# The order of the first stage of an attention-and-FFN kernel: demodulation rows, norms, folded matrix and first value projection against the first scores

## The reference, cut to what matters

```python
x = x * s1[:, None, :]
x = (x - mu) * jax.lax.rsqrt(var + EPS_IN)
q = heads(jnp.einsum('bsh,oh->bso', x, q_weight) * q_dc[:, None, :])
k = heads(jnp.einsum('bsh,oh->bso', x, k_weight) * k_dc[:, None, :])
v_flat = jnp.einsum('bsh,oh->bso', x, v_weight) * v_dc[:, None, :] * s2[:, None, :]
attn = jax.nn.softmax(jnp.einsum('bhqd,bhkd->bhqk', q, k) * scale, axis=-1)
out = jnp.einsum('bhqk,bhkd->bhqd', attn, v).transpose(0, 2, 1, 3).reshape(B, S, H)
out = jnp.einsum('bsh,oh->bso', out, w_weight) * w_dc[:, None, :]
skip = jnp.einsum('bsh,oh->bso', v_flat, u_weight) * u_dc[:, None, :]
return x_in + ffn(out + skip)   # ffn: int8 product with absmax scales
```

## Time and profile before

| what | us |
|---|---|
| median of three runs (lowest, highest) | 430.51 (429.87, 430.66) |
| profiled execution | 430.85 |
| its span | 429.0 |
| PE busy in the span | 406.4 |
| ACT, DVE, POOL busy | 294.9, 279.0, 107.4 |

### The profile page before, as it was taken

How to read it: one execution, slowest core, us unless ns; L and a number is a source line. 1 busy time by engine, 2 the same in 40 slices (tenths; PEclk the granted TensorE clock), 3 DMA queues, 4 the chain that set the end, 5 groups by cost and what they waited for, 6 DMA issues and landing times.

```text
span 429.0 us, 7595 instructions
## 1 busy us (share of the span) xinstructions
PE 406.4 (95%) x2544; PEld 216.7 (51%) x2544; DVE 279.0 (65%) x634; ACT 294.9 (69%) x341; POOL 107.4 (25%) x115
## 2 busy tenths in 40 slices
PE   8886989999999999999999999999999999999894
PEld 7773625354544455454445554445545545453273
DVE  7645468455984778566875588477856656547355
ACT  2533378868777687867786787868786878787811
POOL 7175204100231023500523023502350052102201
PEclk9996889999999999999999999999999999999999
DMA  5399225723475426622586326621773157602021
GB/s 164 111 137 135 26 101 103 132 70 98 72 127 108 107 70 130 170 74 98 113 133 158 99 68 131 174 81 63 141 172 74 37 109 125 163 0 99 2 98 49
DMA packets 29327, 44.19 MB, mean 103 GB/s; under 512 B 3880, under 2 KB 15144, under 8 KB 29256
## 3 DMA queue, kind: packets, MB, share of 16 engines
q1 hardware_dynamic: 27040, 38.31, 40.8%
q0 software_dynamic: 1040, 3.70, 2.7%
q10 hardware_dynamic: 1200, 1.59, 2.4%
HBM read 14.17 MB, written 4.25 MB: 43 GB/s over the span
## 4 chain that ended last, share of the span: by engine, by line
PE 79%; DVE 8%; ACT 4%; DMA 3%; issue 3%; SPq 1%; POOL 0%; DVEq 0%; POOLq 0%
PE o_acc L1088 26%; PE scores L1074 18%; PE work L1139 12%; PE work L1116 8%; PE work L1200 5%; ACT probs L557 4%; DMA k_stack<-parts 2%; PE work L1127 2%; PE work L1355 2%; PE work L1243 1%; DMA rows<-in_cond_dram 1%; SPq L293 1%; PE work L1229 1%; PE work L1215 1%; PE work L1051 1%
## 5 line engine op out<-in xcount | busy, mean ns | idle before, releaser
L557 ACT ACTIVATE probs<-scores 128x1024 f32<-128x1024 f32 x256 | 247.5, 1024 | 82.4 <-PE scores L1074 82.4
L1088 PE MATMUL o_acc<-probs,v_aug 128*32 128x512 f32 x1024 | 124.4, 604 | 0.0
L1074 PE MATMUL scores<-q_stack,k_stack 50*128 50x512 f32 x512 | 98.2, 455 | 8.5 <-ACT probs L557 5.7
L1074 PEld LDWEIGHTS scores<-q_stack,k_stack 50*128 50x128 f32 x512 | 39.9, 186 | 81.0 <-ACT probs L557 63.3
L1088 PEld LDWEIGHTS o_acc<-probs,v_aug 128*32 128x32 f32 x1024 | 26.9, 110 | 60.4 <-issue 57.0
L1139 PE MATMUL work<-vs_w,x_t 128*128 128x512 f32 x192 | 52.9, 420 | 0.0
L438 POOL TENSOR_TENSOR squares<-parts 128x512 bf16<-128x512 f32 x30 | 31.3, 1042 | 68.2 <-ACT parts L541 68.2
L694 DVE TENSOR_TENSOR v_aug<-work,rows 128x128 f32<-128x128 f32 x64 | 15.6, 286 | 45.8 <-PE work L1139 45.2
L1139 PEld LDWEIGHTS work<-vs_w,x_t 128*128 128x128 f32 x192 | 35.7, 196 | 15.9 <-issue 7.2
L1116 PE MATMUL work<-x_t,qk_w 128*128 128x512 f32 x168 | 43.0, 404 | 0.0
L446 POOL TENSOR_TENSOR res<-res,x_res 128x512 f32<-128x512 f32 x15 | 19.1, 1280 | 90.8 <-DVEq L837 90.8
(11 more groups left out here) (161 smaller groups left out, 442.9 us busy)
## 6 DMA issues: line engine op xcount, KB each, us to landing
q_stack<-parts SPq DMA_DIRECT2D x96, 128.0 KB, 3.8
k_stack<-parts SPq DMA_DIRECT2D x88, 128.0 KB, 4.0
x_res<-in_x_dram SPq DMA_DIRECT2D x8, 512.0 KB, 4.4
x_sb<-in_x_dram SPq DMA_DIRECT2D x7, 512.0 KB, 5.1
out_dram<-res POOLq DMA_DIRECT2D x7, 512.0 KB, 4.7
rows<-rows_dram SPq DMA_DIRECT2D x7, 384.0 KB, 4.1
rows<-in_cond_dram SPq DMA_DIRECT2D x8, 128.0 KB, 4.9
k_stack<-parts ACTq DMA_DIRECT2D x8, 128.0 KB, 9.7
```

Source lines behind the costliest of these rows:

```text
L557: nc.scalar.activation(probs[:, r % RING, pair:pair + 2, :], scores[:, pair:pair + 2, :], ACT.Exp).then_inc(exp_done, 1)
L1074: last = nc.tensor.matmul(scores[:, 2 * (u % 2) + e, :], k_stack[top:top + ROWS, t % 2, head, kt * P:(kt + 1) * P], q_stack[top:top + ROWS ...
L1088: last = nc.tensor.matmul(o_acc[DV * j:DV * (j + 1), :], v_aug[:, kt, 4 * g + j, :], probs[:, r % RING, 2 * (j % 2) + j // 2, :], start=(k ...
```

## The change

- PE: the six transposes of `demod` come first, then the dummy matmuls (five, into `o_acc`), then the norms, also in `o_acc`, so that they take no `work` bank. Skip matrix, transposed maximum, `rows_of_first` and `values(0, 0)` follow, all before the flag is read and before the first scores. `values(0, 1)` stands between the scores of rounds 0 and 1, and `values(0, 2)` is all that is left of the fill of step 0.
- ACT: copies the two rows banks (L586 of the new file) in place of DVE. It no longer issues the four DMAs with the high part of k for group 1, and loads the table of the exponential behind the rounding of the skip matrix.
- SP: issues those four DMAs, between the last q loads and the last two k loads of group 1.
- DVE: `modulate(1)` stands between the low parts of group 0 and the sums, `measure()` behind the reciprocal. The maximum of the norms comes before the last low part. The rest of the skip matrix, the copies of batch 0's rows and `v_and_skip(0, 0)` come before the branch. `normalise_x(1)` comes before `v_and_skip(0, 2)`.
- POOL: `inverse_root(1)` comes before the two memsets.

```diff
-        return [[("row", 0, 0), ("row", 0, 1), ("v", t, 0), ("v", t, 1), ("v", t, 2)],
+        return [[("v", t, 0), ("v", t, 1), ("v", t, 2)],
...
-    ORDER = [("cond", 0, 0), ("sums", 0, 0), ("xt", 0, 0), ("xt", 0, 1), ("sums", 0, 1), ("norms", 0, 0), ("fold", 0, 0),
-             ("rows", 0, 0), ("rows", 0, 1)]
+    ORDER = [("cond", 0, 0), ("sums", 0, 0), ("xt", 0, 0), ("xt", 0, 1), ("sums", 0, 1), ("rows", 0, 0),
+             ("rows", 0, 1), ("fold", 0, 0), ("row", 0, 0), ("row", 0, 1)]
...
+        def norms_bank(a):
+
+            return o_acc[:, :] if a == 0 else work[:, USE[("norms", a, 0)] % NW, :]
...
             load_stack(0, 2, 1)
+            load_stack(0, 3, 0)
             load_stack(0, 3, 1)
...
             scale_values(0)
+            inverse_root(1)
             nc.gpsimd.memset(k_stack[:, 1, :, :].bitcast(F32), 1.0).then_inc(k_cleared, 1)
             nc.gpsimd.memset(q_stack[:, 1, :, :].bitcast(F32), 0.0).then_inc(q_cleared[1], 1)
-            inverse_root(1)
...
-            act.wait_ge(hi_ready, 4)
-            act.sem_inc(spare, 1)
-            load_first_keys(3, 0)
-            load_first_keys(3, 2)
-
-            nc.scalar.activation(table[:, :], ones[:, 0:1], ACT.Exp)
+            for n in range(2):
+                use = USE[("rows", 0, n)]
+                act.wait_ge(work_ready, use + 1)
+                ms = slice(0, 2) if n == 0 else slice(2, 3)
+                nc.scalar.activation(demod_rows[:, ms, :], work[0:B, use % NW, 0:(2 - n) * H].rearrange(
+                    "b (m o) -> b m o", m=2 - n), ACT.Copy).then_inc(demod_rows_ready, 1)
+                act.wait_ge(demod_rows_ready, n + 1)
+                act.sem_inc(work_freed, 1)
             use = USE[("fold", 0, 0)]
             act.wait_ge(work_ready, use + 1)
             nc.scalar.activation(vs_w[:, 0, :, H:2 * H], work[:, use % NW, :].rearrange("p (c o) -> p c o", c=HC), ACT.Copy
                                  ).then_inc(first_hi, 1)
+
+            nc.scalar.activation(table[:, :], ones[:, 0:1], ACT.Exp)
...
             low_part(0, 1)
+            modulate(1)
             sums(1, other_chunks)
             dve.wait_ge(root_ready, 2)
             nc.vector.reciprocal(demod[:, other_chunks, :], demod[:, other_chunks, :]).then_inc(inverse_ready, 1)
+            measure()
...
             low_part(0, 2)
+            largest_norms(0)
             low_part(0, 3)
-            largest_norms(0)
             bound_flag(0)
...
-            row_shift(0)
-            modulate(1)
-            measure()
...
             dve.sem_inc(first_rows, 1)
+            v_and_skip(0, 0)
+            row_shift(0)
...
-                    v_and_skip(t, 0)
                     v_and_skip(t, 1)
+                    normalise_x(1)
                     v_and_skip(t, 2)
-                    normalise_x(1)
...
-            pe.wait_ge(work_freed, USE[("norms", 0, 0)] - NW + 1)
-            keep_clock(work[:, USE[("norms", 0, 0)] % NW, :], 6)
-            norms(0)
-            norms_transposed(0)
-            skip_matrix(0)
             pe.wait_ge(demod_ready, 1)
...
-            row_maxima(0, PROLOGUE_USES)
+            pe.wait_ge(wu_ready, 1)
+            keep_clock(norms_bank(0), 5)
+            norms(0)
+            skip_matrix(0)
+            norms_transposed(0)
+            rows_of_first()
+            values(0, 0)
+            row_maxima(0, USE[("v", 0, 0)] + 1)
...
                     scores_of(r)
+                    if r == 0:
+                        values(0, 1)
```

More of the change, by code:

```diff
@@ L1144, in norms @@
                 pe.wait_ge(squares_ready, a * 4 + 4)
-                bank = claim("norms", a, 0)
+                bank = norms_bank(0) if a == 0 else claim("norms", a, 0)
                 for n in range(4):
@@ L1153, in norms_transposed @@
                 pe.wait_ge(norms_ready, a + 1)
-                bank = work[:, USE[("norms", a, 0)] % NW, :]
-                transpose(bank[0:1, 0:P], norm_max[:, :]).then_inc(work_ready, 1)
+                transpose(norms_bank(a)[0:1, 0:P], norm_max[:, :]).then_inc(first_norms if a == 0 else work_ready, 1)
             def row_maxima(a, uses_done):
@@ L1279, in fill @@
                 if i == 0:
-                    if first:
-                        rows_of_first()
-                        values(t, 0)
-                    values(t, 1)
+                    if not first:
+                        values(t, 1)
                     values(t, 2)
```

25 lines of the change are left out of this document (11 added, 14 removed).

## The result

The changed kernel takes 424.18 us in the median of four runs (422.6 to 426.85), the kernel before beside it 430.19 (429.62 to 430.66): a ratio of 0.9856, 95% interval 0.9827 to 0.9885. The median of all nine is 423.26; the forecast was 423.3. That it is met so closely is luck, since single runs lie up to 3.6 us from it and the first four have their median 0.9 above it.

What follows compares the result with a forecast made beforehand. PE bounds the kernel, busy 95% of the span; in the first slices its waits, order and half clock do. Profiled 430.85 less 7.2 gives 423.65; lowered for the profile lying 0.34 above the median: 423.3 us, range 421.3 to 426.8.

Steps and rivals of the forecast that it cites:

- Skip matrix at 29.81: PE's skip matrix keeps its start of 29.81 us, following POOL's scaled wv at 29.50; bounds 0 and +1.
- Rival 1: The clock falls between skip matrix and `values(0, 0)`: most likely 1.65 us lost, 424.9, up to 428.3; chance 0.30.
- Flag and the rest of the skip matrix: Flag written 1.52 us after the transposed maximum starts, at 33.3; rest of skip matrix done at 34.0, `values(0, 0)` at 34.2.
- The branch: PE's flag read and branch ahead of the first scores: 0.1 us, mostly hidden by `values(0, 0)`; bounds 0 and 1.8.
- First scores: First scores on PE start at 35.9 us against 35.08 before, 0.8 later.
- Value matmuls: Value matmuls of round 0 start at 41.2 us instead of 48.36.
- rival 3: First scores late through style row, open branch or group 0's landing: 424.3 to 425.5; sign, scores after 36.5; chance 0.08.
- The sum: Value matmuls of round 0 start 7.2 us earlier, and the whole kernel gains that 7.2 us.
- rival 2: The second half-clock stretch, 59.4 to 62.7 us, vanishes too: 1.6 us more gained, 421.7; chance 0.18.
- The edits that cost nothing: Copies on ACT, table load, one dummy less, `inverse_root(1)`, `normalise_x(1)` and SP's extra DMAs add nothing to the time.
- The four DMAs: Moving ACT's four k loads brings group 0 forward under 0.3 us, landing 34.7 to 35.0, 0.9 ahead of first scores.
- Rival 4: SP's fuller queue delays the store of the rows and x of batch 2, passing the gain on: 432.0; chance 0.05.

Runs made afterwards that it cites:

- warm_before: The kernel before with ten dummy matmuls added behind the transposes of `demod`, in PE's wait for the stacked operands: 431.15 us, ratio 1.0018.
- second execution: Profiled execution of the changed kernel, unedited, from its later measurement on another chip: 422.16 us; that measurement's median 423.07 us, ratio 0.9831.
- queue_undone: The changed kernel with the four high-part k loads of group 1 issued by ACT again: 422.59 us, ratio 0.9837.
- store_flag: The changed kernel with SP storing the rows ahead of the last two k loads, and DVE's flag behind the rest of the skip matrix: 423.62 us, ratio 0.9842.
- order_alone: The kernel before with only the projections reordered, and DVE's copies of batch 0's rows and `v_and_skip(0, 0)` ahead of its branch: 427.9 us, ratio 0.9948.
- between_undone: The changed kernel with `values(0, 1)` again behind the scores of round 1: 424.4 us, ratio 0.9866.
- order_undone: The changed kernel with spread rows and value projections behind the first scores again, and DVE's branch ahead of batch 0's row copies: 431.55 us, ratio 1.0005.
- warm_before_2: The kernel before with ten dummy matmuls behind the transposes of `demod`, the same kernel measured a second time: 429.78 us, ratio 0.9965.
- pauses_undone: The changed kernel with batch 1's `modulate` and `measure` behind DVE's branch again, and `inverse_root(1)` behind the memsets: 422.56 us, ratio 0.9828.

## Why the prediction was right, point by point

- **What bounded the stretch.** Right in kind. Of the time between first scores and value matmuls of round 0, 13.2 us, the new order leaves 5.24. The clock's part, read from rows 4, was tested only in part, since it fell in that test too: 2.6 us by `warm_before`'s trace.
- **Skip matrix at 29.81.** 29.90 in the second execution, 31.09 in the first. That DVE would not make POOL late holds (`modulate(1)` took 1.56 in its new place rather than 1.22, the sums started at 23.47 in the first), but the scaled wv was not what the skip matrix waited for: it was there at 28.55 and 28.79, and PE came late, so that 29.90 is near the forecast by luck. What was missed is a fall of the clock in the projections *before* it. In `queue_undone`, without that fall, the same 12 matmuls took 3.06, and the skip matrix followed POOL's product (to 28.93) at 28.98, 0.8 ahead of the forecast. Rival 1 put the fall between skip matrix and value projection and was given 0.30; there the clock was 1.00 in all nine executions with the change's order and its parts around it. It fell at 22 to 29 instead in three of the nine, at a price of 2.3 us in those 12 matmuls of the first (5.32 less 3.06); its skip matrix came 1.3 later than forecast.
- **Flag and the rest of the skip matrix.** Mis-sized: the flag was written 1.15 us after the transposed maximum's start, not 1.52. `values(0, 0)` began 3.82 after the skip matrix, forecast 4.4. These 0.6 us were won.
- **The branch.** Taken at 0.1 between 0 and 1.8: 0.18. `store_flag` fits the other bound, 1.82 from flag to scores, when the cover is gone.
- **First scores.** Forecast 35.9: 35.58 and, with the slow projections, 36.77. **Behind them** 5.3: 5.24 and 5.22. **Value matmuls** forecast 41.2: 40.82 and 41.99. The first execution shows a sign of rival 3, scores behind 36.5, but for none of its reasons: neither style row nor branch nor DMA was late, the clock was.
- **The sum.** 7.2 forecast; by the chain 6.3 in the first execution (0.9 less: 1.3 lost ahead of the skip matrix, and 0.4 won behind it, the 0.6 of the flag less 0.2 in the branch and in rounding) and 7.5 in the second. Then 0.5 was given back in the first (the value matmuls at 53 took 3.52, those before 3.18, and a few tenths are unaccounted for), while in the second the fall at 53 did not come at all: that is rival 2, and the milestone moved to -8.7. So the 7.2 stand for what runs with different falls of the clock give on average, and not for a sum of which each term came true. Forecast and rival 2 are two draws of one kernel, not two possible kernels.
- **The edits that cost nothing.** They cost nothing, but the text did not say what they are worth. It treated copies on ACT as neutral, when more than half of the sum hung on the parts around the order: with the transposes behind the skip matrix and DVE's copies, the spread rows do not lie in the wait for it, and `order_alone` gets 3.0 us.
- **The four DMAs.** Group 0 of `k_stack` landed about 34.9 in `between_undone`, without ACT's four, and about 34.5 in `queue_undone`, with them; forecast 34.7 to 35.0 (35.37 in `store_flag`). So the queue of the four does not matter, as the sum had it. The margin of 0.9 to the first scores does not always hold: with a skip matrix at 28.98 or 29.31 these two executions have PE ready for the scores as the DMA lands, and `between_undone` waits 0.15 us for it. The 3 to 4 us that the prediction took from the round-robin between queues were misread: ACT's four for group 1 stand on their queue behind its four for group 0, so they could take from SP's queue only what was left once those had moved. In `queue_undone` ACT's queue had moved 0.52 MB, its group 0, by 32 us, at the end 0.13 MB in each 2 us beside 0.13 and 0.12 on SP's; then nothing from 32 to 34, though its last four DMAs were issued by 29.2, beside 0.26 on SP's; then 0.13 again beside 0.14. The equal shares agree with the Trainium skill's rule (DMA: Bandwidth & Descriptors, Queues, rings and completion order) that a DMA engine goes round-robin between the queues that have work. By that rule group 0 would have gained half of the 3 us from 32 to 35, some 1.5 us (an estimate), and not 3 to 4. It gained nothing that shows, since ACT's queue moved next to nothing then (0.02 MB from 32 to 34); no run here shows why.
- **Rival 4.** Out as a threat, as the Trainium skill's rule that spreading DMAs over issuing engines brings no bandwidth would have it (DMA: Bandwidth & Descriptors, Rules for kernel authors). The trace agrees: from 36 to 38 us SP's queue alone moved 0.27 MB in the changed kernel's first trace, SP's and ACT's together 0.26 in the kernel before. The store landed at 46.3 in the second. Present as 0.62 us of PE's time.

## What to carry to other kernels

Work that needs nothing of a late operand belongs ahead of the first instruction that waits for it, and the next such piece between two steps that share buffers with a slower engine; both waits are found by asking what ended PE's idle time. Before such a move is priced, list who makes its inputs and what stands before them on that engine: here the move alone gave 3.0 us, and 6 to 7.8 with the parts around it, of which moving two copies from DVE to an idle ACT is the one that the wait points at. Where a flag is read to a register in front of the next step, as here, some 1.8 us of other work have to cover it; shortening the chain in front of it by pushing the flag back gained nothing.

## What the runs showed of the hardware that was not expected

- The granted clock falls at different places in executions of one program: 12 to 17 in thirteen of fourteen profiles (not in that of the kernel before), 22 to 29 in four, 53 to 57 in four, 69 once, 390 to 402 in four. Most of these places are behind small matmuls or short waits, but the same ones pass at full clock in other executions. No pause is needed: ahead of the fall at 22.7 PE was busy for 2.30 of 2.30 us, with the small matmuls of the sums, and ahead of the one at 38.9 in `warm_before` it had stood still for no more than 0.88 and 0.42. Filling one did not lower the median. What decides between executions, the traces do not show.
- The lower clock starts behind the pause, not in it. In `order_undone` the granted clock was 1.00 through 3.45 us without a matmul and 0.50 for the 9.80 behind them; in `order_alone` the spread rows (34.55, 1.12 us) still ran at the upper level behind an idle 2.46, and the next six matmuls did not. So a pause is paid by the work behind it.
- A stall of PE of 1.21 us at 227 us in `warm_before`, in the middle of 16 equal matmuls (2.1 us for the weight load), with no releaser; ACT, DVE and the DMAs give no cause. None of the other 13 traces has PE idle for 0.5 us or more without a releaser in the first 410 us.
- Reading a flag to a register and branching costs DVE 1.72 to 1.82 us in the five traces where its next work waits for nothing else (the kernel before, `warm_before`, `warm_before_2`, `order_alone`, `pauses_undone`), and the 1.82 of `store_flag` suggests the same on PE.
